# Gated scan with routed experts: the gates' tanh ahead of a ScalarE copy, the turned low parts earlier on VectorE

## The reference, cut to what matters

```python
x = x + attn(layernorm(x)); x = x + ffn(layernorm(x))
# attn: a = tanh(x WA'), b = x WB', g = sigmoid(x Wg' + bg), dx = x WD' + bD
#       h_t = a_t * h_(t-1) + b_t   (16 states)
#       y = (h WC') * g + dx * (1 - g)
# ffn:  shared = (silu(x @ sg) * (x @ su)) @ sd
#       p = softmax(x @ router); best two experts e of each row
#       routed = sum over the two of p_e * ((silu(x @ g_e) * (x @ u_e)) @ d_e)
#       routed + shared
```

## Time and profile before

| what | value |
|---|---|
| median of 3 runs | 698.24 us (696.83 to 698.5) |
| the profiled execution's own time | 697.29 us |
| its span, first to last instruction | 695.5 us |
| busy in the span: PE, PE's weight loads | 612.1 us (88%), 557.1 us (80%) |
| busy in the span: DVE, POOL, ACT | 520.5 us (75%), 415.7 us (60%), 320.3 us (46%) |
| chain that ended last | PE 35%, issue 20%, POOL 20%, DVE 12%, ACT 8%, DMA 3% |

### The profile page before, as it was taken

The page is one execution under the profiler, slowest core; times in us unless marked ns, Lnnn a source line. Parts: engine busy times, 40 slices in busy tenths (PEclk is TensorE's granted clock), DMA queues, the critical chain, the costliest instruction groups (busy, mean ns, idle before and its releaser), DMA issues.

```text
span 695.5 us, 16435 instructions
## 1 busy us (share of the span) xinstructions
PE 612.1 (88%) x4404; PEld 557.1 (80%) x4405; DVE 520.5 (75%) x1574; ACT 320.3 (46%) x647; POOL 415.7 (60%) x525
## 2 busy tenths in 40 slices
PE   1779999999999999999998818999999969999992
PEld 1678998888988898888886708998888868898892
DVE  8767888888898889888888864776676637677672
ACT  5454466645754566546655403343433324343340
POOL 3312765676556755676565761666666646666765
PEclk9988999999999999999999878999999989999997
DMA  7911422343134412841112236777777468878860
GB/s 250 326 47 54 145 68 102 123 146 122 55 115 144 147 50 104 277 165 58 59 70 92 100 119 223 227 228 239 253 219 250 123 188 240 240 214 256 252 206 15
DMA packets 77919, 109.75 MB, mean 158 GB/s; under 512 B 11496, under 2 KB 54814, under 8 KB 77863
## 3 DMA queue, kind: packets, MB, share of 16 engines
q1 hardware_dynamic: 61990, 66.84, 32.3%
q0 software_dynamic: 15872, 42.24, 16.2%
HBM read 58.37 MB, written 54.85 MB: 163 GB/s over the span
## 4 chain that ended last, share of the span: by engine, by line
PE 35%; issue 20%; POOL 20%; DVE 12%; ACT 8%; DMA 3%; POOLq 1%; SPq 1%; DVEq 0%; ACTq 0%
PE zv L414 14%; POOL best_rows L1498 10%; PE tr L408 5%; PE dn L414 5%; POOL second_rows L1492 4%; ACT ring L695 3%; PE gu L414 3%; POOL x_c L1483 2%; DVE states L1196 2%; ACT state_parts L747 2%; PE zv L470 2%; POOL out L1576 2%; DVE act_s L1022 1%; PE cb L408 1%; DVE rstd L934 1%
## 5 line engine op out<-in xcount | busy, mean ns | idle before, releaser
L414 PE MATMUL zv<-w_hi,bx 128*128 x640 | 125.6, 299 | 0.0
L470 PE MATMUL zv<-wgd,xT 128*128 128x256 f32 x768 | 113.7, 302 | 0.0
L1576 POOL DMA_INDIRECT sums<-y,target x80 | 78.6, 982 | 51.7 <-DVE y L1378 25.1
L1576 POOL DMA_INDIRECT out<-y,target x80 | 78.6, 982 | 45.1 <-issue 23.6
L470 PEld LDWEIGHTS zv<-wgd,xT 128*128 128x128 f32 x768 | 103.9, 196 | 1.8
L414 PEld LDWEIGHTS zv<-w_hi,bx 128*128 128x128 f32 x640 | 95.6, 193 | 5.2 <-issue 0.4
L408 PE MATMUL tr<-ident,ring 128*128 128x128 f32 x448 | 67.2, 279 | 30.3 <-DMA ring<-best_rows 15.8
L1498 POOL DMA_INDIRECT best_rows<-ring,slot x64 | 77.5, 1211 | 18.7 <-issue 17.1
L1362 DVE TENSOR_TENSOR bx<-tr,bx 128x512 fp32r<-128x512 f32 x80 | 55.3, 691 | 36.0 <-ACT bx L876 21.1
L876 ACT ACTIVATE bx<-tr 128x512 fp32r<-128x512 f32 x79 | 47.2, 598 | 75.3 <-PE tr L408 75.3
L408 PEld LDWEIGHTS tr<-ident,ring 128*128 128x128 f32 x448 | 51.5, 143 | 34.9 <-issue 30.6
(11 more groups left out here) (209 smaller groups left out, 1454.2 us busy)
## 6 DMA issues: line engine op xcount, KB each, us to landing
ring<-best_rows SPq DMA_DIRECT2D x80, 258.0 KB
ring<-second_rows SPq DMA_DIRECT2D x80, 130.0 KB
ring<-sums SPq DMA_DIRECT2D x80, 128.0 KB, 3.0
xs<-in_x SPq DMA_DIRECT2D x16, 512.0 KB, 3.8
best_rows<-fill_rows SPq DMA_DIRECT2D x2, 2064.0 KB, 15.9
second_rows<-fill_rows SPq DMA_DIRECT2D x2, 1040.0 KB, 11.4
raw_w<-in_gate_w SPq DMA_DIRECT2D x16, 128.0 KB, 3.8
raw_w<-in_up_w SPq DMA_DIRECT2D x16, 128.0 KB, 4.5
```

The costliest lines, as they stand in the source:

```text
L414: last = pe.matmul(dst, lhs(a, c), rhs(b, c), start=m == 0, stop=m == len(steps) - 1)
L470: end = pe.matmul(two[:, h], xT[a][:, c, rows], wgd[b][:, c, at:at + D], start=False, stop=at == 0 and h == 1 and (a, b, c) == (1, 0, KC - 1))
L1576: pool.indirect_dma_start(out=rows, out_offset=bass.IndirectOffsetOnAxis(ap=target[:, r, h:h + 1], axis=0), in_=y[:, r, h, :], in_offset=N ...
```

## The change

Two orders change, one on ACT and one on DVE; no operation is added or taken away.

On ACT, `gates_out(0)` of block f now stands directly behind the tanh of the decays, ahead of `inner_hi(k - 1, 1)`. On DVE, the two xT_rest of half step s move ahead: the first stands behind the four index searches (`best_index`), the second behind the two statistics `y_stats`. `below_best`, `below_second`, `y_means`, `choose`, in three half steps `down_lo`, and the Newton steps now follow them. The Newton steps 0 to 5 stand in one run ahead of `gated_inner(k, 0)`.

```diff
                     act.activation(states[:], misc[0:N, :], ACT.Tanh).then_inc(decay_ready, 1)
+                if front:
+                    gates_out(0)
                 if tail:
                     inner_hi(k - 1, 1)
                 if front:
-                    gates_out(0)
                     act.wait_ge(scanned, f + 1)
...
                 if back:
                     for j in range(J):
                         best_index(j)
+                def xT_rest(g):
+                    dve.wait_ge(xT_hi, 2 * (s + 2) + g + 1)
+                    turned_rest(xT, tr[g], g).then_inc(xT_ready, 1)
+
+                xT_rest(0)
                 y_stats(2)
                 y_stats(3)
+                xT_rest(1)
                 if back:
                     below_best()
                     below_second()
...
-                next_newton(0)
-                next_newton(1)
-                for g in range(2):
-                    dve.wait_ge(xT_hi, 2 * (s + 2) + g + 1)
-                    turned_rest(xT, tr[g], g).then_inc(xT_ready, 1)
-                    next_newton(2 * g + 2)
-                    next_newton(2 * g + 3)
+                for i in range(6):
+                    next_newton(i)
                 if back:
                     gated_inner(k, 0)
                 next_newton(6)
```

## The result

The changed kernel takes 713.46 us, the median of four executions (709.48 to 727.37), and the kernel before takes 697.57 (also four, 696.83 to 698.5). The ratio is 1.0215, with a 95% interval of 1.0195 to 1.0235. So the change makes the kernel 15 us slower, where 1.9 us less had been forecast. The profiled execution took 712.5 us, its span is 710.7 us.

What follows compares the result with a forecast made beforehand. The loop of DVE, ACT and POOL was taken as the bound in steady half steps, not PE. Terms -1.1 + 0.5 - 1.26 gave 695.4 us from the profiled 697.29, or 696.3 against the median 698.24; range 693.2 to 700.0.

Steps and rivals of the forecast that it cites:

- The step that failed: ACT, steady half steps: `gates_out(0)` ends by 244.4, before `inner_hi` can start at 244.52, so moving it ahead costs 0.
- Rival B: Late PE gates make `gates_out(0)` push `inner_hi` and the state copies 0.5 us in each half step: 703.6 us, chance 0.06.
- open Newton gaps: DVE, steady half steps: `gated_inner(k, 0)` starts 0.25 us later, covered by idle time; cost 0, at most 0.05 us each.
- The chance of slower: Chance given to a slower result: 0.09, beside 0.33 for faster and 0.58 for within 0.3%.
- Half step 1: ACT: late PE gates make `gate_t` wait and `inner_hi` and the copies follow later; cost 0.5 us, between 0.3 and 0.7.
- The start: Half step -1: the second xT_rest comes sooner on DVE, so PE starts earlier; gain 1.1 us (1.0 to 1.2).
- Half step 0: DVE waits at the first xT_rest, `gated_inner(0, 0)` about 1 us later; cost 0 by PE's lead, 1 if not covered.
- half steps with `down_lo`: Half steps 6, 9, 12: Newton step 8 gets through before POOL's `inner_lo`; gain 0.42 us each, 1.26 for three.
- Rival C: Newton step 8 doesn't get through in the `down_lo` half steps: +0.75 in place of -1.26, 698.4 us, chance 0.25.
- rival D: Newton gaps of 0.25 us uncovered in 13 half steps, late `inner_lo` holding Newton step 7 longer: 700.9 us, chance 0.07.
- the wait for `odds`: Sign of a right forecast: in steady half steps DVE's wait for POOL's `odds` falls from 1.04 to about 0.8 us.
- Rival A: PE is the bound, so its removed waits and the earlier start save 7.5 us: 690.7 us, chance 0.12.

Runs made afterwards that it cites:

- e8: The changed kernel, with POOL's `x_c(0)` also waiting for DVE's `placed`: 699.74 us, ratio 1.0036 to the kernel before.
- e14: The change's DVE order alone, ACT's order as before, run a second time on another chip: 695.28 us, ratio 0.9972 to the kernel before.
- e4: The kernel before, with DVE's `h2T_rest(1)` moved ahead of `add_shared(1)`: 756.44 us, ratio 0.9981 to the kernel before on the same chip.
- e6: The kernel before, with two unused DVE copies ahead of the places, and POOL's `x_c(0)` also waiting for `placed`: 702.94 us, ratio 1.0088.
- e5: The kernel before, with two unused 128x128 DVE copies that make `placed` about 0.4 us later: 714.18 us, ratio 1.0252.
- e11: The changed kernel, with DVE's four operations of the places ahead of the four ln1 averages, no wait added: 699.07 us, ratio 1.0034.
- e12: The change's DVE order alone, ACT's as before, with the four operations of the places ahead of the averages: 696.25 us, ratio 0.9979.
- e1: The change's ACT order alone, DVE's order as before: 775.84 us, ratio 1.0234 to the kernel before on the same chip.
- e7: The changed kernel, with ACT's old order in half step 1 alone: 704.66 us, ratio 1.0129 to the kernel before.
- e3: The changed kernel, with three extra unused 512-column matmuls of PE ahead of `recurrent(1)`: 765.32 us, ratio 1.0040 to the kernel before on the same chip.

## Why the prediction was wrong, and where it was right

**The step that failed** is the one on ACT in steady half steps: "`gates_out(0)` ... ends by 244.4, before `gated_inner(k - 1, 1)` lets `inner_hi` start at 244.52. So `inner_hi` and the copies at 245.84 stay where they are. Cost: 0." It rested on two things read from one undisturbed half step: PE's gates 0.8 us ahead of the scan (243.79 against 244.59), and a clock that stays at 1.00. Where the clock does stay up, the step holds: in the half steps 2, 3, 6 and 9 of e8 `inner_hi` starts 0.07 or 0.08 us ahead of the scan, and they are as long as in e14, to 0.03 us. But with ACT's new order a late gate pushes `inner_hi`, and behind a fall of the clock the gates are late: e8 has them 0.20 us behind the scan at 153.04, 1.0 later than the rows of before. In the changed kernel they are late in every half step but 2, 7 and 10, which follow the longest ones (24.9 to 25.2 us). With the old ACT order, and DVE's old order too, falls of 3.4 us cost nothing (e4) or at most 0.1 us (half steps 3, 6 and 10 of e6, each behind one), because `inner_hi` stood ahead of the waiting tanh. The kernel before has no fall between 59 and 379 us that could have shown it; but the cost of 0 had the clock as a condition, and that the prediction doesn't say.

**Rival B had the mechanism and the wrong price.** It named the push of `inner_hi` with a margin of 0.23 us and priced it at 0.5 us in each half step, with a chance of 0.06. Nine half steps were held, and such a one costs 23.9 - 22.37 = 1.5 us. By e14, e8 and e5 that is 0.15 for the open Newton gaps, 0.4 for the late gates and 1.0 for the race. The 0.5 was the pitch of the pushed operation, and what it pushes came on top: `inner_lo` onto `state_parts`, `state_parts` onto `placed`, and `placed` behind `x_c`. The prediction used the very rule that prices this, for the Newton steps at `inner_lo`, and didn't ask it of the other operations with two SBUF inputs that stand beside a large one of POOL. The row that mattered most, `placed` 0.21 us ahead of `x_c`, was not read. By the ratios the race is 1.0215 / 1.0036 = 1.018, some 12.5 us, with what it brings along (12 falls of the clock in place of 4); the ACT order itself is another 0.4 to 0.6% (e11 to e12, e8 to e14), and the DVE part takes 0.3% off. The chance of slower should have been several times 0.09.

The Trainium skill (SBUF — State Buffer, "SBUF: two separate sides") states that a DVE operation with two SBUF inputs and a GpSimd operation that reads SBUF take a shared pair of ports exclusively, the first to start keeping it to its end. The traces agree: `placed` 0.19 us behind `x_c` ends 0.15 us after it, 0.21 us ahead it lasts 0.29, and e5 and e6 switch it by order alone.

**Half step 1** was +0.5 (0.3 to 0.7) in the sum. It grew by 2.2 us, from 22.69 to 24.87: `inner_hi` 0.94 behind the scan (0.12 ahead of it before), `state_parts` 1.43, `placed` 1.26. With `placed` free (e8, e11) it is 23.91, so +1.2 without the race: the term was less than half of that, and its range too low.

**The start** was right: -1.1. From `y_sum(1)` to PE's first `wab` it took 36.81 - 33.01 = 3.80 us before and 34.53 - 31.93 = 2.60 after, 1.2 less. All five kernels with DVE's old order have 3.80 or 3.81, all nine with the new one 2.59 or 2.60. That PE started 2.28 us sooner in the changed kernel is scatter in front of it: `y_sum(1)` starts anywhere from 31.93 to 33.45 us in these kernels, whose start is alike. Half step 0, put at 0, hides in such scatter too: from PE's first `wab` to the scan of half step 1 it is 27.59 us before and 27.54 in e14, and 24.0 to 26.8 in the other kernels with the new DVE order.

**The DVE part as a whole** came out near its sum, in part by luck. -1.1 and -1.26 make 2.4 us less, and e14 is 2.0 less by its ratio (0.7 to 3.2). But in the profiled executions e14 is 0.90 us ahead at the scan of half step 1 and 0.87 at the last scan: between them both take 293.2 us, for what the half steps with `down_lo` gain the steady ones give back (the open Newton gaps, below). The three half steps with `down_lo` last 22.73, 22.75 and 22.73 us in place of 23.16, 23.16 and 23.14, the 0.42 that was taken, and for the reason given. Timeline of DVE in half step 6 of e14, beside the earlier trace rows:

```profile
197.69 0.17 DVE L929 TENSOR_TENSOR newton_t<-rstd 128x8 f32<-128x8 f32 x1
198.26 0.69 DVE L1022 TENSOR_TENSOR act_s<-gu,act_s 128x512 f32<-128x512 f32 x1 [0.40 <-ACT act_s L740]
198.87 0.34 DVE L931 SCALAR_TENSOR_TENSOR newton_t<-newton_t,var_eps 128x8 f32<-128x8 f32 x1
199.24 1.21 DVE L1196 TENSOR_TENSOR_SCAN states<-states,misc 16x512 f32<-16x512 f32 x1
```

Newton step 8 gets through ahead of `inner_lo`, and the third row, step 9, is the one that is held. Rival C falls with that.

**The open Newton gaps** were put at 0.25 us, covered, so at 0, and are not quite: steady half steps of e14 last 22.52 us, 0.15 more than before. DVE and POOL in its half step 3, whose scan starts at 108.86, beside the earlier trace rows:

```profile
127.67 0.68 DVE L1022 TENSOR_TENSOR act_s<-cb,act_s 128x512 f32<-128x512 f32 x1
...
129.00 0.58 DVE L1068 RECIPROCAL odds<-odds 128x68 f32<-128x68 f32 x1 [0.58 <-POOL odds L1522]
129.50 0.97 DVE L934 SCALAR_TENSOR_TENSOR rstd<-newton_t,rstd 128x8 f32<-128x8 f32 x1
```

```profile
129.16 1.28 POOL L1489 TENSOR_TENSOR innerT<-act_s,innerT 128x512 fp32r<-128x512 f32 x1 [0.20 <-ACT innerT L706]
```

`gated_inner(k, 0)` starts 18.81 us behind the scan in place of 240.62 - 222.22 = 18.40. So the gaps are 0.4 us and not 0.25; the 0.25 were covered as reckoned, and the 0.15 above them show: `inner_lo` waits 0.20 us for ACT, starts 0.15 later and holds Newton step 7 for 0.97 in place of 0.75. That is rival D at a little over half its price, and the wait for `odds` falls to 0.58 and not to 0.8.

**Rival A** is out. In the changed kernel PE's waits for `xT` and `gate_t` are gone, in e14 those for `gate_t` are 8.4 us in place of 2.2, and e14 is the faster one by 2.4% (1.0215 / 0.9972). The row of e14:

```profile
PE zv L465 <- ACT gate_t L727: 8.4, 11, 0.9
```

In steady half steps the loop of DVE, ACT and POOL sets the length, as said; the longer falls of e5 show where PE does.

## What to carry to other kernels

Where two engines exclude each other, list the pairs of operations that start within a few tenths of a microsecond of each other on the bounding loop, and price a shift at the whole hold of the worst pair and not at the shift: in e5 some 0.4 us of added work, 0.2 more than the margin, became 1.4, of which 1.0 is the hold. Such a kernel is steady only by luck of its margins, so force the order with a wait or give the small operation room; a wait added on the bounding engine took 11 us off. And of two operations on an in-order engine, the one whose input is at times late belongs behind the one whose output the loop needs, even where a steady half step shows them free to change places. That held on ACT for the gates' tanh and on DVE for the low part of `xT`.

## What the runs showed of the hardware

- A 128x128 operation of DVE with two SBUF inputs that lasts 0.29 us lasts 1.25 to 1.43 us when POOL's 128x512 addition starts up to 0.2 us ahead of it, and 0.29 when it starts 0.05 us behind it. At 0.01 us it went either way: half step 7 of e1 lost, half step 7 of e7 won.
- The granted clock falls to 1.2 GHz with PE busy all the time: in e8 PE is busy for all of the 2 us from 140 to 142, and for all of the 4 from 142 to 146, where the clock is down. In the kernel before the same matmuls in the same order ran at 1.00 for 320 us. Held half steps favour a fall (6 of the 8 held ones of e5 have one and none of its other four), and in the changed kernel PE idles some 0.7 us ahead of the router in them; with that gap filled (e3) the held half steps 1, 4 and 8 have none, but 11 and 12 do. The falls of e4, e6 and e8, which have no held half step, show that it isn't needed. What picks the half step stays open.
- A fall of 3.5 us in one half step made the gates of the next some 1.0 us late against the scan, and whether that cost 0, 0.4 or 1.5 us was decided by the order on ACT and by one race on DVE, not by PE. A fall of twice that length cost 1.0 us by PE alone (e5).
